# First attention of a two-layer cross-attention kernel: context halves of chunk 1 later in unit 0, two norms ahead of exponentials, the first addition to X ahead of a low half

## The chip, the cores and the metric

The kernel runs on one core of a Trainium2 chip. The metric is the device time of one execution in microseconds (us), the median of several runs. TensorE multiplies, ScalarE and VectorE work on SBUF and PSUM, GpSimd on SBUF, SyncE issues the DMAs. In the rows of the profile they are PE (PEld: its weight loads), ACT, DVE, POOL and SP.

## The reference, cut to what matters

```python
x = x + xattn0(layernorm(x), ctx, mask)   # 32 q heads, 8 kv heads, d 128, rotary
x = x + ffn0(layernorm(x))                # 4-bit weights
x = x + xattn1(layernorm(x), ctx)         # q and k normalised
x = x + ffn1(layernorm(x))                # routed, 512 wide
# xattn0, per batch of 64 tokens:
#   q, k = rope(x @ wq), rope(ctx @ wk); v = ctx @ wv
#   out = softmax(q k^T / sqrt(128) + mask) v @ wo
```

There are 32 batches of 64 tokens, 2048 tokens of width 512. The change touches the first attention (L = 0) alone.

## The kernel before, in words

Precision is kept by splitting each operand of a matmul into a high f16 part and a low f16 part, what the high part leaves over. Each product is three matmuls (high x high, high x low, low x high), so an output tile of 128 x 512 with depth 512 takes 12 matmuls. ScalarE makes most high parts (a copy with a conversion), VectorE most low parts (a subtraction).

**Units.** The tokens are in four chunks c of 512 (eight batches each), the heads in eight groups g of four query heads and one key and value head. A unit u is a pair (g, c); attention 0 has 32 of them. `UNITS` gives the order: (0,0), (1,0), (0,1), (1,1), (0,2), (1,2), (0,3), (1,3), and from there group by group. So chunk 1 of the context is first used by the keys of unit 2, chunk 2 by unit 4, chunk 3 by unit 6. Chunk c's layer norm is first used by the queries of those units.

**The pipeline.** Everything is written out by hand for each engine, and each engine runs its list strictly in order; semaphores join them. In step u (`units`, one function of this name per engine) the engines do the scores and softmax of unit u, the projections of unit u + 1 (`front(L, u + 1, beside=u)`), the output projection of unit u - 1 and then the weighted values of unit u:

- TensorE (`units`, L1292; `front`, L1277): `scores(u)` L934; `keys(u+1)` L865, `values(u+1)` L877; for each head h of four `queries(u+1, h)` L909; `turn_p` L943 (only for units 0 and 31; other units turn the weights by DMA, from SyncE); for t of four `output(u-1, t)` L957; `weigh(u)` L999.
- ScalarE (`units`, L1901; `front`, L1859): `turned_k` L1517 (halves of the key exchanged for the rotation), `exponent` L1599, `values_0` L1524, `keys_0` L1531, then per head `turned_q` L1538, and with a lag of two heads the high part `queries_0` L1545; `halved_p` L1609 in the middle. `weighed` L1629 at the start of the next step.
- VectorE (`units`, L2713; `front`, L2681): `weighed` L2331, `soft_max_0` L2255 to L2273, `turned_k` L2170, `soft_sum` L2309, `values_0` L2175, `keys_0` L2187, then per head `turned_q` L2182 and, lagging, the low part `queries_0` L2191. After the heads comes, for t of four, `output(u-1, t)` L2346, which adds the output tile in PSUM to X; between these are the low parts of the last two heads.
- GpSimd (`front`, L3090): the rotation's product with the sine L2953 and sum L2958 per head, the normalisation of the softmax L2964, the low parts of the weights L2973.

**Slots.** Other work is laid beside this with `plan(L, u, slot, stage, ...)`. Every engine calls `side(L, u, slot)` at ten fixed places of a step (0 ahead of the heads, 1 to 4 behind head 0 to 3, 5 to 8 behind output tile 0 to 3, 9 at the end), and `side` runs those planned stages that the engine has a part in. A stage name stands for different functions on different engines:

- `scale` of a context chunk or weight: on ScalarE the four high parts (L1480 for contexts, L1505 for weights). `low`: on VectorE two of the four low parts (L2127), for one half. Both read a staging area that one load fills; the next load of that area waits for the last low part.
- `ln_stats`: VectorE's statistics (L2133, L2139) and GpSimd's power and product (L2937, L2939). `ln_norm`: ScalarE writes the normalised rows of two of a chunk's four tiles (L1640). `ln_turn`: TensorE transposes them (L1028) and ScalarE takes the high parts (L1652). `ln_low`: VectorE takes the low parts (L2149).
- `peak`: TensorE, then VectorE find a power of two to scale by.

**PSUM banks.** `bank(i, ...)` makes TensorE wait until the readers of bank i's last content are through. The output tiles t = 0..3 use banks 2, 3, 0, 2, so that tile 3 waits for the addition of tile 0. `weigh` uses banks 0 and 1 first, so that it waits for the addition of tile 2. `ln_turn` uses banks 2 and 3 for the first two tiles of a chunk and 1 and 6 for the others, but for chunk 1 of this attention banks 2 and 3 both times.

In units 2, 4 and 30 (`LN_BESIDE`) ScalarE does the side stages of slot 5 ahead of the high part of head 3.

Of the kernel before, what the change touches and what calls it, by code (L numbers as in the profile page):

```python
# [87 lines left out]
def build(nc, din, out):  # L88
    ctx = ExitStack()
    with ctx:  # L90
# [330 lines left out]
        def plan(L, u, slot, *stage):  # L421
            SIDE.setdefault((L, u, slot), []).append(stage)
# [8 lines left out]
        def plan_ln(L, u, i, c, early=True, last=6):  # L431

            if early:
                plan(L, u - 1, 9, "ln_stats", i, c)
            for half, (norm, turn, low) in enumerate(((0, 2, 2), (3, 5, last))):
                plan(L, u, norm, "ln_norm", i, c, half)
                plan(L, u, turn, "ln_turn", i, c, half)
                plan(L, u, low, "ln_low", i, c, half)
# [6 lines left out]
                                                        ("low", key, 1))):  # L445
                plan(L, u, slot, *stage, *bank)

        for slot, *stage in ((1, "peak", ("c", 1), 2), (2, "scale", ("c", 1)), (2, "low", ("c", 1), 0), (9, "low", ("c", 1), 1)):
            plan(0, 0, slot, *stage)
        for slot, *stage in ((4, "ln_turn", 0), (4, "ln_norm", 1), (5, "ln_low", 0), (9, "ln_turn", 1), (9, "ln_low", 1)):  # L450
            plan(0, 0, slot, stage[0], 0, 1, *stage[1:])
        for u, slot, *stage in ((0, 1, "peak", w(0, 0, 2), 3), (0, 9, "scale", w(0, 0, 2)), (1, 0, "low", w(0, 0, 2), 0),
                                (1, 1, "low", w(0, 0, 2), 1)):
            plan(0, u, slot, *stage)
# [10 lines left out]
        for u in range(8, NU):  # L465
            g, c = UNITS[0][u]
# [6 lines left out]
        for u, slot, name, *a in ((26, 9, "gi", 1, 0), (27, 1, "gi", 1, 1), (27, 3, "gi", 1, 2), (27, 7, "zp", 1, 0), (27, 8, "zp", 1, 1),  # L473
                                  (27, 9, "zp", 1, 2), (28, 1, "zp", 0, 0), (28, 2, "zp", 0, 1), (28, 3, "zp", 0, 2),
                                  (28, 3, "gi", 0, 0), (28, 9, "gi", 0, 1), (29, 0, "gi", 0, 2)):
            plan(0, u, slot, name, *a)
        plan_ln(0, 30, 1, 0, last=7)
        for k, u, slot, hi in ((0, 29, 2, 3), (1, 29, 7, 5), (2, 30, 1, 7), (3, 30, 4, 0)):
            plan(0, u, slot, "unpack", 0, k)
            if hi:  # L480
# [11 lines left out]
        for u in range(8, NU):  # L492
            g, c = UNITS[1][u]
# [962 lines left out]
        def scalar(act):  # L1456
# [402 lines left out]
            def front(L, u, beside):  # L1859

                if L == 0:
                    if u > 1:
                        turned_k(u)
                    exponent(0, beside)
                    if u > 1:
                        values_0(u)
# [198 lines left out]
        def vector(dve):  # L2065
# [615 lines left out]
            def front(L, u, beside):  # L2681
                if (L, u) != (1, 1):
                    unit_scale(L, u)
                if L == 0:
                    if u > 1:
                        turned_k(u)
                    soft_sum(0, beside)
                    if u > 1:
                        values_0(u)
                    keys_0(u)  # L2690
                    side(0, beside, 0)
                    for h in range(4):
                        turned_q(u, h)
                        if (beside, h) == (0, 3):
                            turned_p(0, 0)
                        if h == 2:
                            halved_p(0, beside, 1)
                        if h in (2, 3):
                            queries_0(u, h - 2)
                        side(0, beside, 1 + h)  # L2700
                else:
                    if beside > 0:
                        values_1(u, 0)
                        soft_sum(1, beside)
                        values_1(u, 1)
                    else:
                        soft_sum(1, 0)
                    side(1, beside, 0)
                    for h in range(4):
                        queries_1(u, h)  # L2710
                        side(1, beside, 1 + h)

            def units(L):  # L2713
                for u in range(NU - 1):
# [13 lines left out]
                    for t in range(4):  # L2728
                        if u > 0:
                            output(L, u - 1, t)  # L2730
                        if L == 0 and t == 0:
                            queries_0(u + 1, 2)
                        if L and t == 1 and not k_by_dma(1, u + 1):
                            keys_1(u + 1)
# [529 lines left out]
```

## Time and profile before

| | us |
|---|---|
| median of 3 runs (2399.04 to 2400.89) | 2399.43 |
| the profiled execution | 2399.88 |
| its span, first to last instruction | 2398.1 |
| TensorE busy | 2349.9 |
| VectorE busy | 1740.3 |
| GpSimd busy | 1298.6 |
| ScalarE busy | 1290.0 |
| attention 0, until the last `weigh` of its steps | 0 to 965 |

The mean granted TensorE clock is 0.995 of 2.4 GHz. A row of the timeline has start (us from the span's start), duration of the merged group, engine, line, operation, what it writes and reads, count, and in brackets the idle time of the engine ahead of it with what released it. L numbers are those of the kernel before.

### The profile page before, as it was taken

How to read it: one execution, taken by the hardware profiler on the slowest of the kernel's cores; microseconds unless marked ns; L12 is line 12 of the kernel's file. 1: busy time of each engine (PE TensorE's matmuls, PEld its weight loads, DVE VectorE, ACT ScalarE, POOL GpSimd, SP SyncE). 2: the span in 40 equal slices, each digit the busy share in tenths (PEclk: the TensorE clock that was granted, in tenths of full speed). 3: DMA queues.
4: the chain of work that ended last, by engine and by line, in shares of the span. 5: the costliest groups of instructions: out<-in, count | busy, mean ns of one | idle time of the engine just before them, and what ended most of it. 6: DMA issues, size and time to landing. Idle time of an engine off the chain costs nothing.

```text
span 2398.1 us, 46211 instructions
## 1 busy us (share of the span) xinstructions
PE 2349.9 (98%) x18020; PEld 1329.5 (55%) x18028; DVE 1740.3 (73%) x3256; ACT 1290.0 (54%) x2511; POOL 1298.6 (54%) x1042
## 2 busy tenths in 40 slices
PE   8899999999999999999989999999999999999998
PEld 4555555555555555444666555555555555555554
DVE  8887887878787898756777576667666666766666
ACT  7666665656555555424444564555555555554453
POOL 4656566666666566237853354445555555445541
PEclk9999999999999999999999999999999999999999
DMA  6111121312121111011102111122121212221101
GB/s 213 45 45 36 45 54 27 124 27 54 32 56 29 43 40 29 27 44 36 35 21 69 58 32 28 45 54 63 36 63 36 63 36 62 54 43 27 27 14 71
DMA packets 217913, 116.60 MB, mean 49 GB/s; under 512 B 169409, under 2 KB 192609, under 8 KB 216673
## 3 DMA queue, kind: packets, MB, share of 16 engines
q1 hardware_dynamic: 217696, 113.64, 18.7%
q8 instruction: 145, 2.38, 0.4%
q14 instruction: 72, 0.58, 0.1%
HBM read 65.81 MB, written 8.39 MB: 31 GB/s over the span
## 4 chain that ended last, share of the span: by engine, by line
PE 55%; DVE 5%; ACT 2%; issue 1%; POOL 1%; DMA 0%; DVEq 0%; SPq 0%; ACTq 0%; POOLq 0%
PE PB L957 16%; PE PB L909 14%; PE PB L893 6%; PE PB L1069 4%; PE PB L1126 4%; PE PB L1080 3%; PE PB L934 2%; PE PB L999 2%; PE PB L978 1%; PE PB L1028 1%; DVE SML L2133 0%; PE PB L1223 0%; PE PB L1179 0%; DVE X L2489 0%; DVE X L2346 0%
## 5 line engine op out<-in xcount | busy, mean ns | idle before, releaser
L957 PE MATMUL PB<-WB,AR 128*128 128x512 f16 x3072 | 682.7, 379 | 2.5 <-DVE X L2346 2.3
L909 PE MATMUL PB<-XTB,WB 128*128 128x512 f16 x3072 | 678.9, 379 | 2.6 <-DVE WB L2127 1.5
L957 PEld LDWEIGHTS PB<-WB,AR 128*128 128x128 f16 x3072 | 296.7, 98 | 356.9 <-DVE X L2346 6.6
L909 PEld LDWEIGHTS PB<-XTB,WB 128*128 128x128 f16 x3072 | 297.5, 98 | 346.6 <-issue 6.2
L2964 POOL TENSOR_TENSOR AR<-AR,SML 128x512 f32<-128x512 f32 x128 | 144.7, 1152 | 314.4 <-DVE SML L2316 314.4
L2346 DVE SCALAR_TENSOR_TENSOR X<-PB,SML,X 128x512 f32<-128x512 f32 x256 | 188.9, 747 | 165.0 <-PE PB L957 159.0
L1629 ACT ACTIVATE AR<-PB 128x512 f16<-128x512 f32 x256 | 131.5, 598 | 231.7 <-PE PB L999 231.6
L2953 POOL TENSOR_TENSOR AR<-AR,CST 128x512 f32<-128x512 f32 x128 | 191.0, 1492 | 31.6 <-ACT AR L1539 31.6
L2220 DVE TENSOR_TENSOR AR<-PB,AR 128x512 f16<-128x512 f32 x128 | 88.2, 690 | 164.4 <-ACT AR L1592 164.4
L2958 POOL TENSOR_TENSOR AR<-AR 128x512 f32<-128x512 f32 x128 | 177.1, 1384 | 11.7 <-DVE AR L2182 1.9
L2944 POOL TENSOR_TENSOR AR<-AR,CST 128x512 f32<-128x512 f32 x32 | 46.7, 1460 | 237.3 <-ACT AR L1518 237.3
L1545 ACT ACTIVATE AR<-AR 128x512 f16<-128x512 f32 x128 | 80.7, 631 | 175.1 <-POOL AR L2958 173.6
L893 PE MATMUL PB<-WB,CTB 128*128 128x256 f16 x1536 | 173.1, 273 | 0.1
L2331 DVE TENSOR_TENSOR AR<-PB,AR 128x512 f16<-128x512 f32 x256 | 158.7, 683 | 13.3 <-ACT AR L1629 13.2
L2182 DVE TENSOR_TENSOR AR<-PB,CST 128x512 f32<-128x512 f32 x128 | 88.2, 689 | 107.6 <-ACT AR L1539 107.5
L3002 POOL TENSOR_TENSOR SML<-SML 128x16 f32<-128x16 f32 (+1 forms) x33 | 98.2, 2976 | 120.7 <-DVE SML L2228 120.7
L2191 DVE TENSOR_TENSOR AR<-AR 128x512 f16<-128x512 f32 x128 | 144.3, 1128 | 23.9 <-ACT AR L1545 23.9
L893 PEld LDWEIGHTS PB<-WB,CTB 128*128 128x128 f16 x1536 | 148.2, 98 | 17.4 <-DVE X L2346 0.4
L2994 POOL TENSOR_TENSOR AR<-AR 128x512 bf16<-128x512 f32 x128 | 146.9, 1157 | 16.1 <-ACT AR L1592 16.0
L2973 POOL TENSOR_TENSOR PSP<-AR,PSP 128x512 f16<-128x512 f32 x93 | 118.8, 1290 | 0.0
L934 PE MATMUL PB<-AR 128*128 128x64 f16 x3072 | 102.9, 194 | 3.2 <-DVE AR L2191 2.0
L934 PEld LDWEIGHTS PB<-AR 128*128 128x128 f16 x3072 | 95.7, 98 | 15.9 <-issue 14.3
(313 smaller groups left out, 4120.6 us busy)
## 6 DMA issues: line engine op xcount, KB each, us to landing
STG<-in_wo SPq DMA_DIRECT2D x14, 1024.0 KB
STG<-in_wq SPq DMA_DIRECT2D x13, 1024.0 KB
STG<-in_qw_gu SPq DMA_DIRECT2D x40, 128.0 KB
STG<-in_ctxT SPq DMA_DIRECT2D x4, 1024.0 KB
X<-in_x SPq DMA_DIRECT2D x4, 1024.0 KB, 10.4
kept<-CTB SPq DMA_DIRECT2D x4, 1024.0 KB, 7.3
CTB<-kept SPq DMA_DIRECT2D x4, 1024.0 KB, 6.4
out_x<-X SPq DMA_DIRECT2D x16, 256.0 KB, 2.4
```

The costliest lines, as they stand in the source:

```text
L893: m = pe.do.matmul(b[:, t2 * 256:(t2 + 1) * 256], CT[x][c][:, k, tok], wkv[y][:, k, :], start=n == 0, stop=n == 11)
L909: m = pe.do.matmul(b[:, :], wq[x][:, k, h * 128:(h + 1) * 128], XT[y][c][:, k, :], start=n == 0, stop=n == 11)
L934: m = pe.do.matmul(bk[:, b * SQ:(b + 1) * SQ], rows_of(QT[x], pair, b), KTT[y][:, b * SQ:(b + 1) * SQ], start=n == 0 and not by_pe, stop=n ...
L957: m = pe.do.matmul(b[:, :], AT[x][:, h, t * 128:(t + 1) * 128], wo[y][:, h, :], start=n == 0, stop=n == 11)
L1629: act.do.activation(hi, b[:, :].rearrange("p (b h q) -> p b h q", b=2, h=4), copy).then_inc(at_hi.of((L, u, j, odd)), 1)
L2191: dve.do.tensor_tensor(head_of(QT[1], h), by_batch(M1[h]), head_of(QT[0], h), ALU.subtract).then_inc(q_lo.of((0, u, h)), 1)
L2331: dve.do.tensor_tensor(lo, b[:, :].rearrange("p (b h q) -> p b h q", b=2, h=4), hi, ALU.subtract).then_inc(at_lo.of((L, u, j, odd)), 1)
L2346: dve.do.scalar_tensor_tensor(xs, PB[WB_OUT[t]][:, :], co(L, u, 0), xs, ALU.mult, ALU.add).then_inc(x_add.of((L, u, t)), 1)
L2953: pool.do.tensor_tensor(rt, rt, SINT.unsqueeze(1).to_broadcast([128, BC, SQ]), ALU.mult).then_inc(q_sin.of((u, h)), 1)
L2958: pool.do.tensor_tensor(M1[h], M1[h], RT[h], ALU.add).then_inc(q_add.of((u, h)), 1)
L2964: pool.do.tensor_tensor(v, v, RCT[:, cols].unsqueeze(2).to_broadcast([128, BC, SQ]), ALU.mult).then_inc(p_n.of((L, u, pair)), 1)
L2994: pool.do.tensor_tensor(head_of(SQL, h), by_batch(M1[h]), head_of(SQH, h), ALU.subtract).then_inc(sql.of((u, h)), 1)
```

## The change

Four edits, all in attention 0, none of which adds or removes an instruction:

1. In step 0 the high parts of context chunk 1 go from slot 2 to slot 4 (ScalarE; there behind `ln_turn` and `ln_norm`), and its first two low parts from slot 2 to slot 5 (VectorE; there behind `ln_low(0,1,0)`). The other two stay in slot 9.
2. The first `ln_norm` of chunks 2 and 3 (steps 2 and 4) goes from slot 0 to a new place "k" that only ScalarE has, ahead of `exponent`.
3. On VectorE, in steps 1 to 30, the low part of query head 1 goes from behind head 3 to behind `output(u-1, 0)`. In step 0, which has no output, it stays.
4. The second `ln_low` of the next norm (1, chunk 0) goes in step 30 from slot 7 to a new place "added" that only VectorE has, right behind `output(29, 0)`.

```diff
--- before.py
+++ after.py
@@ -432,7 +432,7 @@
 
             if early:
                 plan(L, u - 1, 9, "ln_stats", i, c)
-            for half, (norm, turn, low) in enumerate(((0, 2, 2), (3, 5, last))):
+            for half, (norm, turn, low) in enumerate((("k" if L == 0 and u < 5 else 0, 2, 2), (3, 5, last))):
                 plan(L, u, norm, "ln_norm", i, c, half)
                 plan(L, u, turn, "ln_turn", i, c, half)
                 plan(L, u, low, "ln_low", i, c, half)
@@ -445,10 +445,12 @@
                                                         ("low", key, 1))):
                 plan(L, u, slot, *stage, *bank)
 
-        for slot, *stage in ((1, "peak", ("c", 1), 2), (2, "scale", ("c", 1)), (2, "low", ("c", 1), 0), (9, "low", ("c", 1), 1)):
+        for slot, *stage in ((1, "peak", ("c", 1), 2), (9, "low", ("c", 1), 1)):
             plan(0, 0, slot, *stage)
         for slot, *stage in ((4, "ln_turn", 0), (4, "ln_norm", 1), (5, "ln_low", 0), (9, "ln_turn", 1), (9, "ln_low", 1)):
             plan(0, 0, slot, stage[0], 0, 1, *stage[1:])
+        plan(0, 0, 4, "scale", ("c", 1))
+        plan(0, 0, 5, "low", ("c", 1), 0)
         for u, slot, *stage in ((0, 1, "peak", w(0, 0, 2), 3), (0, 9, "scale", w(0, 0, 2)), (1, 0, "low", w(0, 0, 2), 0),
                                 (1, 1, "low", w(0, 0, 2), 1)):
             plan(0, u, slot, *stage)
@@ -474,7 +476,7 @@
                                   (27, 9, "zp", 1, 2), (28, 1, "zp", 0, 0), (28, 2, "zp", 0, 1), (28, 3, "zp", 0, 2),
                                   (28, 3, "gi", 0, 0), (28, 9, "gi", 0, 1), (29, 0, "gi", 0, 2)):
             plan(0, u, slot, name, *a)
-        plan_ln(0, 30, 1, 0, last=7)
+        plan_ln(0, 30, 1, 0, last="added")
         for k, u, slot, hi in ((0, 29, 2, 3), (1, 29, 7, 5), (2, 30, 1, 7), (3, 30, 4, 0)):
             plan(0, u, slot, "unpack", 0, k)
             if hi:
@@ -1861,6 +1863,7 @@
                 if L == 0:
                     if u > 1:
                         turned_k(u)
+                    side(0, beside, "k")
                     exponent(0, beside)
                     if u > 1:
                         values_0(u)
@@ -2695,8 +2698,9 @@
                             turned_p(0, 0)
                         if h == 2:
                             halved_p(0, beside, 1)
-                        if h in (2, 3):
-                            queries_0(u, h - 2)
+                            queries_0(u, 0)
+                        if h == 3 and beside == 0:
+                            queries_0(u, 1)
                         side(0, beside, 1 + h)
                 else:
                     if beside > 0:
@@ -2729,6 +2733,9 @@
                         if u > 0:
                             output(L, u - 1, t)
                         if L == 0 and t == 0:
+                            side(0, u, "added")
+                            if u > 0:
+                                queries_0(u + 1, 1)
                             queries_0(u + 1, 2)
                         if L and t == 1 and not k_by_dma(1, u + 1):
                             keys_1(u + 1)
```

## Rows read from the trace of the kernel before

**Rows 1.** The page: TensorE's busy time, and the costliest group of matmuls.

```profile
PE 2349.9 (98%) x18020; PEld 1329.5 (55%) x18028; DVE 1740.3 (73%) x3256; ACT 1290.0 (54%) x2511; POOL 1298.6 (54%) x1042
...
L957 PE MATMUL PB<-WB,AR 128*128 128x512 f16 x3072 | 682.7, 379 | 2.5 <-DVE X L2346 2.3
```

**Rows 2.** Timeline of TensorE, step 0 (columns as told above).

```profile
66.78 2.74 PE L999 MATMUL PB<-AR 64*128 64x256 f16 x24 [4.37 <-DVE AR L2321]
70.19 1.97 PE L1028 MATMUL PB<-CST,LNB 128*128 128x128 f32 x8 [0.67 <-DVE XTB L2149]
...
75.15 2.75 PE L865 MATMUL PB<-CTB,WB 128*128 128x512 f16 x12
```

**Rows 3.** Windows: length; busy us (x) of PE, PEld, DVE, ACT, POOL; granted clock; DMA.

```profile
65.30:75.50 10.20, 7.83 (x83) 6.44 (x85) 7.88 (x12) 7.84 (x14) 5.21 (x4) 0.53 0.08 15
119.90:123.30 3.40, 3.40 (x13) 1.59 (x12) 1.38 (x2) 3.31 (x7) 2.64 (x3) 0.59 0.00 0
```

**Rows 4.** Timeline of TensorE, steps 1 to 3.

```profile
101.94 1.49 PE L999 MATMUL PB<-AR 64*128 64x256 f16 x24 [0.53 <-DMA AR<-PSP]
...
118.71 1.79 PE L1028 MATMUL PB<-CST,LNB 128*128 128x128 f32 x8 [2.34 <-ACT LNB L1640]
...
141.29 2.75 PE L865 MATMUL PB<-CTB,WB 128*128 128x512 f16 x12
```

**Rows 5.** Timeline of TensorE, step 4.

```profile
181.60 1.33 PE L1028 MATMUL PB<-CST,LNB 128*128 128x128 f32 x8 [0.30 <-ACT LNB L1640]
```

**Rows 6.** Waits of TensorE in attention 0 (total, times, longest); step 8, TensorE and VectorE.

```profile
PE PB L957 <- DVE X L2346: 2.3, 5, 1.0
...
317.09 1.48 PE L999 MATMUL PB<-AR 64*128 64x256 f16 x24
...
311.77 1.54 DVE L2191 TENSOR_TENSOR AR<-AR 128x512 f16<-128x512 f32 x1
...
314.91 1.40 DVE L2346 SCALAR_TENSOR_TENSOR X<-PB,SML,X 128x512 f32<-128x512 f32 x2
```

**Rows 7.** Timeline of TensorE, step 30.

```profile
963.61 1.49 PE L999 MATMUL PB<-AR 64*128 64x256 f16 x24 [2.22 <-issue]
```

**Rows 8.** Timeline of ScalarE, step 0.

```profile
58.40 2.56 ACT L1480 ACTIVATE CTB<-STG,SML 128x512 f16<-128x512 f32 x4 [0.48 <-DVE SML L2095]
...
64.11 1.09 ACT L1616 ACTIVATE AR<-PB 128x512 f16<-128x512 f32 x2
...
66.56 1.53 ACT L1640 ACTIVATE LNB<-X,SML 128x512 f32<-128x512 f32 x2
...
72.69 2.55 ACT L1505 ACTIVATE WB<-XTB,SML 128x512 f16<-128x512 f32 x4
```

**Rows 9.** Timeline of VectorE, step 0.

```profile
59.84 3.32 DVE L2127 SCALAR_TENSOR_TENSOR CTB<-STG,SML,CTB 128x512 f16<-128x512 f32 x2
...
65.36 1.27 DVE L2321 TENSOR_TENSOR AR<-PB,AR 128x512 f16<-128x512 f32 x2
...
69.46 1.27 DVE L2149 TENSOR_TENSOR XTB<-PB,XTB 128x512 f16<-128x512 f32 x2
...
71.97 1.41 DVE L2127 SCALAR_TENSOR_TENSOR CTB<-STG,SML,CTB 128x512 f16<-128x512 f32 x2
...
75.75 2.48 DVE L2331 TENSOR_TENSOR AR<-PB,AR 128x512 f16<-128x512 f32 x4 [1.18 <-ACT AR L1629]
```

**Rows 10.** Timeline of GpSimd, steps 0 and 2.

```profile
59.66 1.28 POOL L2958 TENSOR_TENSOR AR<-AR 128x512 f32<-128x512 f32 x1
...
110.57 0.20 POOL L2939 TENSOR_TENSOR SML<-SML 128x4 f32<-128x4 f32 x1
```

**Rows 11.** Timeline of ScalarE, step 2.

```profile
114.50 1.34 ACT L1599 ACTIVATE AR<-AR,SML 128x512 f32<-128x512 f32 x2 [4.68 <-DVE AR L2273]
```

**Rows 12.** Timeline of VectorE, steps 2 and 30.

```profile
138.85 1.40 DVE L2127 SCALAR_TENSOR_TENSOR CTB<-STG,SML,CTB 128x512 f16<-128x512 f32 x2
...
960.15 1.40 DVE L2346 SCALAR_TENSOR_TENSOR X<-PB,SML,X 128x512 f32<-128x512 f32 x2
```

## The prediction

> **What bounds the kernel now.** I read the page's busy shares first: TensorE is busy for 98% of the span [rows 1]. So an edit can only bring what TensorE waits for, and what runs at a low clock. Then TensorE's waits by unit. Attention 0 is a chain of units; in a steady one TensorE waits for nothing, so VectorE, ScalarE and GpSimd count only where TensorE stands behind them. In reach of the change that is in five places. Unit 0: `weigh(0,0)` waits 4.37 us for VectorE's low half of the turned weights, and until the keys of chunk 1 the clock is low [rows 2, 3]. Unit 1: 0.53 us for the transposes, which end that unit's chain of softmax and GpSimd [rows 4]. Unit 2: 2.34 us for the norm of chunk 2, with a low clock behind it [rows 3, 4]. Unit 4: 0.30 us for the norm of chunk 3 [rows 5]. Five later units: 2.3 us together where the fourth output tile waits for the first addition to X, whose bank it takes [rows 6]. Unit 30 has 2.22 us at `weigh` [rows 7].
>
> **1. Context halves of chunk 1, unit 0.** ScalarE's four high parts (2.56 us) [rows 8] leave slot 2 for slot 4, two of VectorE's low parts (3.32 us) [rows 9] for slot 5. No instruction is added. What follows in ScalarE's queue then moves up, but only to where GpSimd's sum of head 0 ends, 60.94 [rows 10]; rotation 3 goes 61.6 to 62.8 and the turned weights start at 62.85 instead of 64.11 [rows 8]. VectorE no longer carries 3.32 us of halves, takes its two subtractions (1.27) [rows 9] behind the first copy, and ends them at 64.75 instead of 66.63: `weigh(0,0)` starts 1.9 us earlier.
>
> That is not where unit 0 ends. ScalarE's high parts now stand between `ln_norm(0,1,1)`, which ended at 68.09 [rows 8] and now ends near 66.9, and the high part of query head 2. They run to 69.4, that head's high part is ready near 70.05 instead of 68.6, and VectorE, idle since about 65.3, makes its low part to 70.7. Behind it in the queue stands `ln_low(0,1,0)`, which before began at 69.46 [rows 9]: now 70.7. TensorE's second turn of the norm (70.19 before) [rows 2] waits for the bank that the first tile frees: 71.5. From there to `keys(2)` were 4.96 us [rows 2]; with the wait for the second bank a little less: 76.2 instead of 75.15, **+1.05**. VectorE meanwhile: halves 0 (1.41, the row of the same two instructions with GpSimd idle) [rows 9], head 3, halves 1, `ln_low`, done by 76.4. ScalarE turns the norm once TensorE has (73.5), to 74.2, then writes `wo`'s high parts (2.55, at 72.69 before) [rows 8] from 74.1, so `weighed` starts near 76.6 and VectorE's four subtractions at 77.1 instead of 75.75 [rows 9]: **+1.4**. They are followed without a gap by the softmax of unit 1, GpSimd's normalisation and the transposes for which `weigh(0,1)` already waited 0.53. TensorE, 1.05 late, has no slack of 1.4: unit 1 ends **1.4 us later**. Bounds: 0, if TensorE's turn runs at full clock and the wait at GpSimd's sum closes; +3.3, if the moved halves still take 3.32. SyncE's next load of that staging area (chunk 2) leaves some 2 us later, ahead of unit 1's transposes; its first reader is ScalarE's square in slot 9 of unit 1, so this costs nothing.
>
> Two instructions of low parts took 3.32 us beside GpSimd and 1.41 us with GpSimd idle [rows 9, 10], and this is why I take 1.41 behind 71.9, where GpSimd has nothing. The Trainium skill (SBUF — State Buffer, "Who interferes with whom") says that a VectorE instruction with two inputs in SBUF and a GpSimd instruction that reads SBUF exclude each other. By that rule the moved halves are free of it (+1.4); without it they would stay at 3.32 and the unit at +3.3.
>
> **2. Norms ahead of exponentials, units 2 and 4.** Two activations (1.53 us) [rows 8] go ahead of exponentials for which ScalarE stood idle 4.68 us in unit 2 [rows 11]; GpSimd has the statistics ready by 110.8 [rows 10], so the norm ends at 112.3, before 114.50, and costs nothing. TensorE's turn is at hand at 116.4 and no longer waits 2.34; without that stall the stretch of 3.40 us at a mean clock of 0.59 (levels 1.2 and 2.4 GHz) [rows 3] should go: 3.40 x 0.41 = 1.4. On TensorE 3.7 us. Next late is VectorE: its queue starts 1.4 us earlier (ScalarE has 1.5 less ahead of the rotations). Walking its queue in the order of the code, with the durations that it had, I get the low parts of chunk 2 done at 138.6, where they ended at 140.25 [rows 12]. `keys(4)` needs them and began at 141.29 [rows 4]; TensorE would be there at 137.6. So **-2.7**, between -1.7 (if VectorE gives 0.65 of its 1.65) and -3.7. Unit 4: the wait of 0.30 and the gap between its two tiles (the turn took 1.33 there [rows 5]): **-0.7**, -0.3 to -0.9; ScalarE is idle ahead of those exponentials too.
>
> **3. First addition ahead of a low half, 30 units; unit 30.** VectorE makes the addition before the low half of head 1 (1.54) [rows 6], so the bank is free 1.5 us earlier. All five waits, 2.3 us [rows 6], go, and each gives back an overlap of 379 - 222 = 157 ns (682.7 us over 3072) [rows 1]: at most 3.1. But `weigh` needs the third addition, which does not move: in the unit with the longest wait (1.0) it ended at 316.31, and `weigh` came at 317.09 [rows 6], so that only 0.7 of 1.2 comes back. The short ones bring 1.8, less 0.6 in units where the third addition is by then just in time: **-1.9**, -0.9 to -3.1. VectorE would stall only where it reached the addition before TensorE ended the first output tile. In that unit three tiles of 12 matmuls, 8.0 us, and the wait lie between that and 317.09: it ended near 308.0, and VectorE comes to the addition at 311.8 [rows 6], 3.8 us after. In unit 30 the profile names no releaser; by the code `weigh` waits there for the bank that the second `ln_low` empties. That comes 4 us earlier now, but pushes back the third addition, for whose bank `weigh` waits too: it ended at 961.55 [rows 12], and with two `ln_low` (1.27) and one low half ahead and head 3 behind it comes near 963.3, against `weigh` at 963.61 [rows 7]: **-0.1**, +0.5 to -0.8.
>
> Sum: 1.4 - 2.7 - 0.7 - 1.9 - 0.1 = **-4.0 us**. The profiled execution took 2399.88 (span 2398.1); the median of the three runs shown is 0.45 lower, 2399.43. So 2395.4. A measurement of this kernel can tell about 0.2%, 4.8 us, from no change: the line lies at 2394.6, close by.
>
> **Rivals.** (a) *VectorE closes up*: chunk 2's low parts are ready when TensorE comes, and all five waits go. For it: the same pair of VectorE instructions takes 1.41 or 3.32 us [rows 9], by what GpSimd does, so its queue may shorten by more than I give it. Against: GpSimd's own queue moves along with it. 1.4 - 3.7 - 0.9 - 3.1 - 0.5 = -6.8: **2392.6**. (b) *Unit 0 costs more*: halves still stretched, or the low clock lasts into the keys, +3.3: sum -2.1, **2397.3**. For it: between TensorE's last transpose near 62.4 and 71.5 there is only one `weigh`. (c) *The gain moves to the third addition*: nothing from part 3: -2.1, **2397.3**. (d) *The other side: slower.* The place is VectorE's wait for TensorE's first output tile, in each of 29 units, with the low halves of heads 1 and 2 queued behind it and the next scores behind those. If it stalls 0.3 us per unit beyond what VectorE's gaps take, that is 8.7, and -4.0 + 1.9 + 8.7 = +6.6: **2406.0**. It decides from a stall of some 0.24 us per unit. Against: the 3.8 us above. (e) *It doesn't do what it says*: the norm of unit 2 doesn't run before the exponentials, because its statistics (VectorE, then GpSimd) are late; they had 3.7 us to spare [rows 10, 11]. Without part 2's gain in unit 2: -1.3, **2398.1**.
>
> **How the numbers follow.** Forecast 0.52, within 1.5 us of it; (a) 0.18, (b) 0.12, (c) 0.09, (d) 0.05, (e) 0.04. The forecast is its likeliest case's: 2395.4. The range reaches to (a) with its bounds below and to (b) and (c) above, leaves out (d), and takes in the spread of the runs shown: 2392.4 to 2398.6. Faster by over 0.2% is (a) and a third of the forecast's own spread: 0.36; within it 0.59; slower 0.05.
>
> **What would show it.** In unit 0 `weigh` starts near 64.9, TensorE then stands about 4 us ahead of the second turn, `weigh(0,1)` near 103.3. In unit 2 the wait for the norm is gone, the clock stays full, and a new wait of about 1 us ahead of `keys(4)` names VectorE's context halves. No wait of an output tile for an addition is left in attention 0, and `weigh` in the unit of 317 waits for one instead. I'm wrong if unit 1 ends earlier than before, if `keys(4)` doesn't wait, or if the gain shrinks steadily from unit 5 to unit 30.

## The result, and the profile after

The changed kernel takes 2407.55 us (2406.46 to 2408.6, 6 runs) against 2399.61 (2398.88 to 2400.89, 6 runs) for the one before on the same chip: ratio 1.0029, 95% interval 1.0019 to 1.0039. That is 8 us slower, where I forecast 4.0 us faster. The profiled execution took 2408.49 with a span of 2406.7, against 2399.88 and 2398.1.

The page's busy times of the kernel after:

```profile
PE 2352.1 (98%) x18028; PEld 1330.1 (55%) x18028; DVE 1759.1 (73%) x3256; ACT 1289.9 (54%) x2511; POOL 1284.5 (53%) x1042
```

VectorE is the row to look at against [rows 1]: the same 3256 instructions are busy for 1759.1 us instead of 1740.3. Instructions that were only moved have become longer. What TensorE waits for up to 975 us (total, times, longest):

```profile
PE PB L1001 <- DVE X L2349: 12.2, 16, 1.6
PE PB L1030 <- DVE XTB L2152: 4.8, 1, 4.8
...
PE PB L1001 <- DVE AR L2324: 1.6, 1, 1.6
...
PE PB L867 <- DVE CTB L2130: 0.6, 1, 0.6
```

(In the kernel after, `weigh` is L1001, `output` L959 and VectorE's addition L2349, its low half L2194, `queries` L911, `keys` L867, `ln_turn` L1030.) The wait of [rows 6], an output tile for the first addition, is gone, as meant. In its place `weigh` waits in 16 units for an addition, 12.2 us together. The groups of instructions say which of VectorE's have grown (busy us, mean ns of one). The query heads' low halves of the kernel before:

```profile
L2191 DVE TENSOR_TENSOR AR<-AR 128x512 f16<-128x512 f32 x128 | 144.3, 1128 | 23.9 <-ACT AR L1545 23.9
```

and of the kernel after:

```profile
L2194 DVE TENSOR_TENSOR AR<-AR 128x512 f16<-128x512 f32 x128 | 168.6, 1332 | 17.8 <-ACT AR L1547 17.6
```

They alone are 24.3 us more. GpSimd is busy for 14.1 us less than before (1284.5 against 1298.6 [rows 1]): part of the time for which one engine held up the other has moved from GpSimd's instructions into VectorE's. Unit 18, a steady one, shows how. VectorE and GpSimd of the kernel before:

```profile
601.59 1.53 DVE L2191 TENSOR_TENSOR AR<-AR 128x512 f16<-128x512 f32 x1
...
603.40 0.75 DVE L2346 SCALAR_TENSOR_TENSOR X<-PB,SML,X 128x512 f32<-128x512 f32 x1
604.07 0.74 DVE L2191 TENSOR_TENSOR AR<-AR 128x512 f16<-128x512 f32 x1
604.73 1.40 DVE L2346 SCALAR_TENSOR_TENSOR X<-PB,SML,X 128x512 f32<-128x512 f32 x2
...
602.54 1.72 POOL L2953 TENSOR_TENSOR AR<-AR,CST 128x512 f32<-128x512 f32 x1
604.34 1.61 POOL L2958 TENSOR_TENSOR AR<-AR 128x512 f32<-128x512 f32 x1
...
607.17 1.05 PE L999 MATMUL PB<-AR 64*128 64x256 f16 x16
```

and of the kernel after:

```profile
606.10 0.75 DVE L2349 SCALAR_TENSOR_TENSOR X<-PB,SML,X 128x512 f32<-128x512 f32 x1
606.77 3.40 DVE L2194 TENSOR_TENSOR AR<-AR 128x512 f16<-128x512 f32 x2
610.09 1.40 DVE L2349 SCALAR_TENSOR_TENSOR X<-PB,SML,X 128x512 f32<-128x512 f32 x2
...
606.69 1.27 POOL L2960 TENSOR_TENSOR AR<-AR,CST 128x512 f32<-128x512 f32 x1
608.03 1.59 POOL L2965 TENSOR_TENSOR AR<-AR 128x512 f32<-128x512 f32 x1
...
611.55 0.72 PE L1001 MATMUL PB<-AR 64*128 64x256 f16 x10 [0.89 <-DVE X L2349]
```

Before, the low half of head 1 runs beside GpSimd (1.53), then the addition stands in between, and the low half of head 2 starts at 604.07, just before GpSimd changes from one instruction to the next (its product ends at 604.26, its sum starts at 604.34). It takes 0.74, and GpSimd's sum behind it 1.61. After, the two follow each other from 606.77, while GpSimd is busy from 606.69 to 609.62 without a gap, and take 3.40 together instead of 2.27. Twenty of the 30 units have such a pair of 3.4 us. From the end of the last rotation product the third addition ends 5.75 us later (605.74 to 611.49) instead of 4.54 (601.59 to 606.13), though the same instructions stand between them. That is 1.21 us, and the third addition had been only 1.04 early (606.13 against 607.17).

How long such a subtraction takes can be told from where it starts. I take the low halves that start more than 0.15 us before the end of a GpSimd instruction: in 92 of 93 cases in the kernel before, and in 89 of 90 in the kernel after, the low half lasts what that instruction still had to run, plus 0.54 to 0.56 us. The two of unit 18 above started with some 1.2 us of a GpSimd instruction to run, and took 1.73 and 1.75.

The 1.21 against 1.04 us would leave a wait of 0.17, and `weigh` waits 0.89. The other 0.7 come from unit 17, whose third addition was late too. VectorE starts the softmax work of unit 18 about 0.5 us later behind `weigh` of unit 17 than before, and a pair of subtractions in it, which are not low halves, meets GpSimd in another way. Before and after:

```profile
585.16 1.29 DVE L2273 TENSOR_TENSOR AR<-AR,SML 128x512 f32<-128x512 f32 x2
...
589.10 1.84 DVE L2276 TENSOR_TENSOR AR<-AR,SML 128x512 f32<-128x512 f32 x2
```

Before, the pair starts 0.06 us after a GpSimd instruction, and that one is held up (2.48 us). After, it starts 0.58 us behind it, GpSimd takes 1.27, and the pair is stretched. Counted from `weigh` of unit 17 (578.20 before, 581.62 after) the pair ends 1.07 us later than before, ScalarE's exponentials start 1.07 later, and the last rotation product ends 0.73 later.

Time from `weigh` to `weigh`, from the timelines, against what I forecast:

| | before | after | difference | forecast |
|---|---|---|---|---|
| start of `weigh` of unit 1 | 101.94 | 104.59 | +2.65 | +1.4 |
| unit 2 | 36.09 | 33.41 | -2.68 | -2.7 |
| unit 3 | 29.40 | 30.13 | +0.73 | 0 |
| unit 4 | 31.85 | 31.09 | -0.76 | -0.7 |
| unit 5 | 28.97 | 28.97 | 0 | 0 |
| units 6 to 29 | 700.88 | 708.29 | +7.41 | -1.9 |
| unit 30 | 34.48 | 33.59 | -0.89 | -0.1 |
| rest of the span | 1434.5 | 1436.6 | +2.1 | 0 |

(The row of a unit is the time from the `weigh` before to its own.) Unit 4 came as forecast. Unit 2 came to the forecast figure, but not in the forecast way: see edit 2 alone, below. TensorE of the kernel after, step 0 and step 2:

```profile
66.44 1.49 PE L1001 MATMUL PB<-AR 64*128 64x256 f16 x24 [1.59 <-DVE AR L2324]
72.69 1.97 PE L1030 MATMUL PB<-CST,LNB 128*128 128x128 f32 x8 [4.76 <-DVE XTB L2152]
...
118.88 0.60 PE L1030 MATMUL PB<-CST,LNB 128*128 128x128 f32 x4
120.54 0.63 PE L1030 MATMUL PB<-CST,LNB 128*128 128x128 f32 x4 [1.06 <-issue]
...
138.00 1.48 PE L1001 MATMUL PB<-AR 64*128 64x256 f16 x24 [0.36 <-DVE X L2349]
...
141.99 1.24 PE L867 MATMUL PB<-CTB,WB 128*128 128x512 f16 x5 [0.57 <-DVE CTB L2130]
```

In step 2 the turn no longer waits 2.34 for ScalarE [rows 4], but its second tile comes 1.06 behind the first, for which the profile names no releaser, and `keys(4)` waits 0.57 for the context halves. This `keys(4)` stands behind `weigh` of unit 2, so its delay is in the row of unit 3: from 138.00 to 141.99 are 3.99 us, from 138.03 to 141.29 before 3.26. In step 0 the wait ahead of `weigh` fell from 4.37 to 1.59, and 4.76 appeared at the second turn. Unit 1 needs care: `turn_p` of unit 0, ahead of all that was moved, stands at 62.94 instead of 60.50, so that execution is 2.4 us late before the change can act. How much of this reaches `weigh` of unit 1, whose wait at the `weigh` before takes up part of it, is worked out below. TensorE was at its low clock at another moment in that execution (from 58 to 68 us at a mean of 1.00 of 2.4 GHz, where the one before had 0.83).

### The profile page after: what moved, and what is told of

The parts are those of the page before. It is cut to its first block, busy times and chain, and to the rows that moved or that the text cites. A ratio compares the mean times of both kernels' runs of the same rounds, so it can differ in the third digit from the quotient of the medians.

```text
span 2406.7 us, 46219 instructions
## 1 busy us (share of the span) xinstructions
PE 2352.1 (98%) x18028; PEld 1330.1 (55%) x18028; DVE 1759.1 (73%) x3256; ACT 1289.9 (54%) x2511; POOL 1284.5 (53%) x1042
## 4 chain that ended last, share of the span: by engine, by line
PE 53%; DVE 5%; ACT 2%; POOL 1%; issue 1%; DMA 0%; DVEq 0%; SPq 0%; ACTq 0%; POOLq 0%
PE PB L959 15%; PE PB L911 13%; PE PB L895 6%; PE PB L1071 4%; PE PB L1128 4%; PE PB L1082 3%; PE PB L936 2%; PE PB L1001 2%; PE PB L980 1%; PE PB L1030 1%; DVE SML L2136 0%; PE PB L1225 0%; PE PB L1181 0%; DVE X L2349 0%; DVE X L2492 0%
## 5 line engine op out<-in xcount | busy, mean ns | idle before, releaser
L911 PE MATMUL PB<-XTB,WB 128*128 128x512 f16 x3072 | 680.2, 380 | 2.3 <-DVE WB L2130 1.2
L959 PE MATMUL PB<-WB,AR 128*128 128x512 f16 x3072 | 681.5, 379 | 0.2
L959 PEld LDWEIGHTS PB<-WB,AR 128*128 128x128 f16 x3072 | 297.5, 98 | 352.6 <-issue 2.6
L911 PEld LDWEIGHTS PB<-XTB,WB 128*128 128x128 f16 x3072 | 297.7, 98 | 347.0 <-issue 7.4
L2349 DVE SCALAR_TENSOR_TENSOR X<-PB,SML,X 128x512 f32<-128x512 f32 x256 | 188.4, 745 | 162.0 <-PE PB L959 156.0
L2960 POOL TENSOR_TENSOR AR<-AR,CST 128x512 f32<-128x512 f32 x128 | 179.2, 1400 | 29.7 <-ACT AR L1541 29.7
L2194 DVE TENSOR_TENSOR AR<-AR 128x512 f16<-128x512 f32 x128 | 168.6, 1332 | 17.8 <-ACT AR L1547 17.6
L2951 POOL TENSOR_TENSOR AR<-AR,CST 128x512 f32<-128x512 f32 x32 | 44.3, 1384 | 252.5 <-ACT AR L1520 252.5
L1001 PE MATMUL PB<-AR 64*128 64x256 f16 x1536 | 95.1, 270 | 14.7 <-DVE X L2349 12.2
```

What stands on the lines that cost most here:

```text
L911: m = pe.do.matmul(b[:, :], wq[x][:, k, h * 128:(h + 1) * 128], XT[y][c][:, k, :], start=n == 0, stop=n == 11)
L959: m = pe.do.matmul(b[:, :], AT[x][:, h, t * 128:(t + 1) * 128], wo[y][:, h, :], start=n == 0, stop=n == 11)
L1001: m = pe.do.matmul(bk[odd][:, jj * 256:(jj + 1) * 256], vd[x][rows, b2, :], PT[y][rows, :, b2, :], start=n == 0, stop=n == 2)
L2194: dve.do.tensor_tensor(head_of(QT[1], h), by_batch(M1[h]), head_of(QT[0], h), ALU.subtract).then_inc(q_lo.of((0, u, h)), 1)
L2349: dve.do.scalar_tensor_tensor(xs, PB[WB_OUT[t]][:, :], co(L, u, 0), xs, ALU.mult, ALU.add).then_inc(x_add.of((L, u, t)), 1)
L2960: pool.do.tensor_tensor(rt, rt, SINT.unsqueeze(1).to_broadcast([128, BC, SQ]), ALU.mult).then_inc(q_sin.of((u, h)), 1)
```

## Experiments

**Which edit costs it.** Theory A: VectorE and GpSimd exclude each other, and edit 3 lets one more low half meet GpSimd. The first four kernels are parts of the change; the kernel before took 2400.4 us beside them.

Edit 3 alone:

```diff
-                        if h in (2, 3):
-                            queries_0(u, h - 2)
+                        if h == 2:
+                            queries_0(u, 0)
+                        if h == 3 and beside == 0:
+                            queries_0(u, 1)
...
                         if L == 0 and t == 0:
+                            if u > 0:
+                                queries_0(u + 1, 1)
                             queries_0(u + 1, 2)
```

> Edit 3 alone: the first addition to X ahead of the low half of head 1, everything else as before. Theory A (VectorE takes the low halves of heads 1 and 2 back to back while GpSimd works, both are stretched, and the third addition, for whose bank weigh waits, comes about 1 us later): +7 us against before (+5.5 to +9), with some 15 waits of weigh for an addition, 11 to 13 us in total, and VectorE's low halves of query heads at a mean of 1.33 us instead of 1.13. Rival B (the loss is made in steps 0 to 2 and by the clock at both ends, and edit 3 only shows it): within 2 us of before. Rival C (VectorE stalls for the first output tile): slower too, but with idle time of VectorE ahead of the first addition in most steps, and no longer low halves.

Measured: 2409.64 us (2408.57 to 2410.38, 5 runs), ratio 1.0035 (1.0022 to 1.0049). Its group of low halves:

```profile
L2191 DVE TENSOR_TENSOR AR<-AR 128x512 f16<-128x512 f32 x128 | 169.6, 1340 | 15.3 <-ACT AR L1545 15.3
```

and, of TensorE's waits, that of `weigh` for an addition:

```profile
PE PB L999 <- DVE X L2346: 10.1, 14, 1.4
```

Units 6 to 29 take 708.14 together. The loss is 9.2 us, a little more than the 5.5 to 9 expected, with a little less of the waits (10.1 us where I expected 11 to 13). This edit holds the whole loss. It does not yet say by what mechanism.

Edits 1, 2 and 4, without edit 3 (against the changed kernel):

```diff
-                            queries_0(u, 0)
-                        if h == 3 and beside == 0:
-                            queries_0(u, 1)
+                        if h in (2, 3):
+                            queries_0(u, h - 2)
...
-                            if u > 0:
-                                queries_0(u + 1, 1)
                             queries_0(u + 1, 2)
```

> The change without edit 3: context halves, norms, and the norm's second low half in step 30. Theory A: what the changed kernel gained in steps 2, 4 and 30 (2.7 + 0.8 + 0.9) stays and steps 5 to 29 cost nothing, against some 1.4 to 2.6 lost in steps 0 and 1: -2 us against before (-4 to 0), and the five waits of an output tile for an addition are back. Rival B: +1 to +3, because the loss is in these edits.

Measured: 2398.67 us (11 runs: ten from 2396.43 to 2400.03, and one of 7362.43), ratio 0.9989 (0.998 to 0.9998). Low halves 142.7 us (mean 1116 ns), units 6 to 29 700.85: as before the change. Step 2 takes 32.98 here, step 3 29.40.

Edit 1 alone:

```diff
-        for slot, *stage in ((1, "peak", ("c", 1), 2), (2, "scale", ("c", 1)), (2, "low", ("c", 1), 0), (9, "low", ("c", 1), 1)):
+        for slot, *stage in ((1, "peak", ("c", 1), 2), (9, "low", ("c", 1), 1)):
...
+        plan(0, 0, 4, "scale", ("c", 1))
+        plan(0, 0, 5, "low", ("c", 1), 0)
```

> Edit 1 alone: the context halves of chunk 1 later in step 0. Forecast's own term: +1.4 us (0 to +3.3), weigh of step 0 up to 1.9 us earlier, the second turn of the norm 1.3 later with a wait of 4 to 5 us ahead of it, weigh of step 1 later by 1.4. Rival: the whole 2.65 us by which weigh of step 1 was late in the changed kernel is edit 1's: +2.65. A second rival: most of it was where the low clock fell, ahead of the moved work: +0.5 or less.

Measured: 2402.58 us (2401.82 to 2405.98, 11 runs), ratio 1.0012 (1.0003 to 1.002). That is 2.2 us slower, with `weigh` of unit 1 at 103.48, 1.5 later than before.

Edit 2 alone:

```diff
-            for half, (norm, turn, low) in enumerate(((0, 2, 2), (3, 5, last))):
+            for half, (norm, turn, low) in enumerate((("k" if L == 0 and u < 5 else 0, 2, 2), (3, 5, last))):
...
+                    side(0, beside, "k")
                     exponent(0, beside)
```

> Edit 2 alone: the norms of chunks 2 and 3 ahead of the exponentials of steps 2 and 4. Theory: step 2 shorter by 2.7 us (36.09 to about 33.4) with a wait of 0.5 to 1 us for the context halves ahead of the keys of unit 4, step 4 by 0.7; -3.4 us against before (-2.4 to -4.6). Rival: VectorE's queue gives the time back in step 3: -1.5 or less.

Measured: 2397.46 us (2395.36 to 2399.45, 11 runs), ratio 0.9987 (0.9978 to 0.9996). Step 2 takes 32.98, step 4 31.09: -3.1 and -0.8. The wait of 0.5 to 1 us ahead of the keys of unit 4 that I expected did not come, neither here nor in the kernel without edit 3. TensorE in step 2 and at `keys(4)`, with edit 2 alone:

```profile
117.69 0.60 PE L1028 MATMUL PB<-CST,LNB 128*128 128x128 f32 x4
119.35 0.63 PE L1028 MATMUL PB<-CST,LNB 128*128 128x128 f32 x4 [1.06 <-issue]
...
139.64 2.75 PE L865 MATMUL PB<-CTB,WB 128*128 128x512 f16 x12
```

So edit 2 alone brings 3.1 us, and TensorE does not wait for VectorE's context halves, which end at 139.41. The wait of 0.57 at `keys(4)` and that of 0.36 at `weigh` of unit 2 are there only with edit 3 beside it, whose low halves of heads 1 and 2 together take 3.05 us in that unit.

**By what mechanism.** The next kernels take an instruction away from GpSimd, or change only VectorE's order; the kernel before took 2400.6 us beside them. In the first two GpSimd's product of head 3 with the sine is left out in units 2 to 31 (they leave this term of the rotation out):

```diff
+                if h == 3 and u > 1:
+                    return
                 pool.do.tensor_tensor(rt, rt, SINT.unsqueeze(1).to_broadcast([128, BC, SQ]), ALU.mult).then_inc(q_sin.of((u, h)), 1)
...
-                pool.wait_ge(q_sin, (u, h))
+                if h < 3 or u < 2:
+                    pool.wait_ge(q_sin, (u, h))
```

With edit 3:

> Edit 3, and GpSimd's product with the sine of head 3 is left out in the units 2 to 31 of the first attention (that head's queries are rotated wrongly). Theory A: only one of the two low halves behind the first addition still starts while GpSimd works, the third addition comes about 1 us earlier than with edit 3 alone, and the waits of weigh for an addition fall from 10 to 12 us to under 2. Against the kernel before +0 us (-3 to +2). Rival C (the order of the additions against TensorE's tiles sets it, not GpSimd): the waits stay at 8 us or more.

Measured: 2396.12 us (2393.65 to 2399.45, 11 runs), ratio 0.9984 (0.9975 to 0.9992). This is 4.5 us faster, more than the 3 at most that I expected; one wait of `weigh` for an addition is left in units 2 to 30, of 0.56.

Without edit 3:

> The kernel before with the same product of GpSimd left out (that head's queries are rotated wrongly), to compare the run above with. Theory A: -1 to -4 us against before; edit 3 on top of it costs at most 2 us where it cost 8.4 on the whole kernel. Rival C: edit 3 costs some 8 us on top of it all the same.

Measured: 2398.73 us (2397.07 to 2400.3, 11 runs), ratio 0.9992 (0.9983 to 1.0001). With one GpSimd instruction fewer, edit 3 brings 2.6 us where it cost 9.2 with that instruction (2409.64 against 2400.4). The intervals of the two ratios overlap, so that the gain is not sure, but a loss of 9 is excluded. In the profiles units 6 to 29 take 697.99 against 699.21 here, and 708.14 against 700.88 with the instruction. Unit 18 of the kernel with edit 3 and less GpSimd:

```profile
600.43 0.75 DVE L2346 SCALAR_TENSOR_TENSOR X<-PB,SML,X 128x512 f32<-128x512 f32 x1
601.10 2.34 DVE L2191 TENSOR_TENSOR AR<-AR 128x512 f16<-128x512 f32 x2
603.36 1.40 DVE L2346 SCALAR_TENSOR_TENSOR X<-PB,SML,X 128x512 f32<-128x512 f32 x2
...
599.79 2.50 POOL L2965 TENSOR_TENSOR AR<-AR 128x512 f32<-128x512 f32 x2
...
605.98 1.27 PE L999 MATMUL PB<-AR 64*128 64x256 f16 x20
```

The same two low halves in the same order take 2.34 us instead of 3.40, because GpSimd is done at 602.29. So it is GpSimd that stretches them, not their order or ScalarE: the first starts with 1.19 us of a GpSimd instruction to run and takes 1.74, the second takes 0.68.

Now the order alone, with all of GpSimd's work: VectorE adds the first tile, makes the low half of head 1, adds the second and third tile, and makes the low halves of heads 2 and 3 last. In step 0, which has no output tiles, this order also puts `ln_low(0,1,0)` and whatever else is in slot 5 ahead of the low half of head 2. The expectation of the kernel with all four edits, below, says "in units 1 to 30" and passes over this. Against edit 3 alone:

```diff
                                 queries_0(u + 1, 1)
-                            queries_0(u + 1, 2)
...
                         if L == 0 and t == 2:
+                            queries_0(u + 1, 2)
                             queries_0(u + 1, 3)
```

> Edit 3 with the low half of head 2 also moved, behind the third addition (VectorE: first addition, low half 1, second and third addition, low halves 2 and 3). Theory A: the third addition is ready some 1.7 us earlier than with edit 3 and no longer late; the low half of head 2 then runs when GpSimd is through, 0.68 us instead of 1.7. Neither weigh nor an output tile waits for an addition: -3 us against before (-4 to 0). Rival: VectorE now stands at the third addition until TensorE's tile is there, ends the step later, and the wait goes to the scores or to the next step's queries: +1 or more.

Measured: 2398.77 us (2396.24 to 2400.94, 11 runs), ratio 0.9993 (0.9984 to 1.0001). Its unit 18:

```profile
600.20 0.75 DVE L2346 SCALAR_TENSOR_TENSOR X<-PB,SML,X 128x512 f32<-128x512 f32 x1
600.86 1.75 DVE L2191 TENSOR_TENSOR AR<-AR 128x512 f16<-128x512 f32 x1
602.53 1.47 DVE L2346 SCALAR_TENSOR_TENSOR X<-PB,SML,X 128x512 f32<-128x512 f32 x2
603.92 1.28 DVE L2191 TENSOR_TENSOR AR<-AR 128x512 f16<-128x512 f32 x2
...
602.14 1.60 POOL L2962 TENSOR_TENSOR AR<-AR 128x512 f32<-128x512 f32 x1
```

and its group of low halves:

```profile
L2191 DVE TENSOR_TENSOR AR<-AR 128x512 f16<-128x512 f32 x128 | 143.4, 1139 | 3.6 <-ACT AR L1545 3.6
```

The low half of head 1 is still stretched (1.75). The additions, which read one operand from PSUM, stand beside GpSimd and take 1.47 for two; the low halves come when GpSimd is done and take 1.28 for two. No wait of TensorE's for an addition is left in units 5 to 29, at an output tile or at `weigh` (one of 0.2 us is left, at a `keys`), and units 6 to 29 take 697.76 together, 3.12 less than before: the upper end that I had given part 3. The whole kernel's median shows 1.8 of the 3 that were expected, and the interval does not exclude none. In the profiled execution unit 30 took 0.5 longer (34.96) and the rest of the span 2.1 (1436.6). That rest lies anywhere between 1434.5 and 1437.7 us in the thirteen profiled executions. TensorE's program is the same in all of them there. Some of the spread can be read right at its start: from `weigh` of unit 30 to the next output tile TensorE takes 3.04 us in most, 4.4 in three that run partly at the low clock there (this one, edit 3 alone, edit 2 alone: 0.88 over the 14 us behind that `weigh`), and 4.02 in the three executions further below that have this order and edit 4 together, where that tile waits 1.03 for VectorE. What sets the remainder stays open.

That order with edits 2 and 4 beside it, without edit 1 (against the kernel above):

```diff
-            for half, (norm, turn, low) in enumerate(((0, 2, 2), (3, 5, last))):
+            for half, (norm, turn, low) in enumerate((("k" if L == 0 and u < 5 else 0, 2, 2), (3, 5, last))):
...
-        plan_ln(0, 30, 1, 0, last=7)
+        plan_ln(0, 30, 1, 0, last="added")
...
+                    side(0, beside, "k")
...
+                            side(0, u, "added")
```

> The order of VectorE above with edits 2 and 4 of the change and without edit 1 (context halves as before). If the parts add up: -3 from the norms, -1 from step 30, -3 from the additions: -7 us against before (-4 to -9), faster than both kernels. Rival (they share one slack): no better than the norms alone, -3.

Measured: 2392.85 us (2390.93 to 2395.03, 6 runs), ratio 0.9965 (0.9953 to 0.9977). This beats both kernels. Unit 30 takes 32.63, 1.85 less than before, and `weigh` waits for nothing there; 1.0 of that is lost again to the wait of 1.03 behind it. The same kernel was measured a second time, beside the two that follow, where the kernel before took 2401.0 us.

> The kernel with edits 2 and 4 and the order addition 0, low half 1, additions 1 and 2, low halves 2 and 3, once more with more runs: its first measurement was 2392.85, ratio 0.9965 (0.9953 to 0.9977), from 6 runs. If that holds, 2391.5 to 2394; if it was a lucky draw, 2395 or above, since the terms give 2400 - 2.7 - 0.7 - 3.1 - 0.9 = 2392.6.

Measured: 2394.3 us (2392.53 to 2395.07, 8 runs), ratio 0.9973 (0.9963 to 0.9983). The gain is there a second time, 6.7 us after 7.7; the median lies between my two cases, just above the first.

All four edits with that order (against the kernel above):

```diff
-        for slot, *stage in ((1, "peak", ("c", 1), 2), (2, "scale", ("c", 1)), (2, "low", ("c", 1), 0), (9, "low", ("c", 1), 1)):
+        for slot, *stage in ((1, "peak", ("c", 1), 2), (9, "low", ("c", 1), 1)):
...
+        plan(0, 0, 4, "scale", ("c", 1))
+        plan(0, 0, 5, "low", ("c", 1), 0)
```

> All four edits of the change, but in units 1 to 30 VectorE's order is addition 0, low half of head 1, additions 1 and 2, low halves of heads 2 and 3, so that the low halves no longer meet more of GpSimd's instructions than before and the third addition is not held up. Theory A (the loss sits in the order of VectorE alone, and the other edits keep what they brought): the kernel with edits 2 and 4 and this order took 2392.85, and edit 1 cost +1.0 to +1.2 where it could be read: 2394, between 2392 and 2396; no wait of weigh for an addition in units 5 to 29, steps 6 to 29 at 697.8 together. Rival B (edit 1 pays once VectorE's queue is no longer the late one): 2392 or below, unit 1 ending no later than 102.2. Rival C (part of the loss comes with edit 1 through VectorE's queue): 2398 or above.

Measured: 2393.44 us (2391.95 to 2394.62, 8 runs), ratio 0.9971 (0.996 to 0.9981), units 6 to 29 at 697.77. Against the changed kernel it differs only by where VectorE's low half of head 2 stands, and the loss of 8 us is a gain of 7.6. The profiled executions are 14.8 us apart: 10.5 of it is in units 6 to 29, and 3.0 ahead of `weigh` of unit 1. For the latter the order in step 0 counts. VectorE and TensorE there:

```profile
66.48 1.27 DVE L2152 TENSOR_TENSOR XTB<-PB,XTB 128x512 f16<-128x512 f32 x2
68.46 2.69 DVE L2130 SCALAR_TENSOR_TENSOR CTB<-STG,SML,CTB 128x512 f16<-128x512 f32 x2 [0.71 <-ACT CTB L1482]
...
68.54 1.27 PE L1030 MATMUL PB<-CST,LNB 128*128 128x128 f32 x8
```

`ln_low(0,1,0)` no longer stands behind the low half of head 2, and the second turn follows `weigh` without the 4.76. The moved context halves meet GpSimd and take 2.69 instead of 1.40. Rival C falls. Of rival B the sign in unit 1 came (101.57, not later than 102.2) with the order in step 0, and the time did not (2392 or below). With edit 1 this order takes 0.9 us less than without it (2394.3), which these runs don't tell apart.

Edit 4 alone:

```diff
-        plan_ln(0, 30, 1, 0, last=7)
+        plan_ln(0, 30, 1, 0, last="added")
...
+                            side(0, u, "added")
```

> Edit 4 alone: the second ln_low of chunk 0 for attention 1 is made behind the first addition of unit 30 in place of slot 7. Forecast of the prediction -0.1 (+0.5 to -0.8); with edits 1 and 2 beside it, step 30 took 33.57 against 34.48. Theory A: step 30 takes 33.6 here too, and the kernel 0.9 less than the one before, which the runs can't tell from none. Rival: step 30 stays at 34.5, and the 0.9 came with the others' later position of the low clock.

Measured: 2399.37 us (2398.17 to 2402.8, 11 runs), ratio 0.9994 (0.9986 to 1.0003). Unit 30 takes 33.60: 0.9 less than before, as theory A had it.

## Why the prediction was wrong

**The step that failed** is in part 3: "`weigh` needs the third addition, which does not move". It moves. The unit that I took this from, with `weigh` at 317.09, shows it after the change:

```profile
312.97 3.42 DVE L2194 TENSOR_TENSOR AR<-AR 128x512 f16<-128x512 f32 x2
316.31 1.40 DVE L2349 SCALAR_TENSOR_TENSOR X<-PB,SML,X 128x512 f32<-128x512 f32 x2
...
317.76 1.48 PE L1001 MATMUL PB<-AR 64*128 64x256 f16 x24 [1.41 <-DVE X L2349]
```

The third addition ends at 317.71 where I had it at 316.31; only 0.18 of this is there ahead of the additions, at VectorE's last rotation product. I had assumed that instructions which change places within a queue leave the sum of their durations alone. Here one of the two low halves was short (0.73) only because the addition between them carried it to the end of a GpSimd instruction. In units 6 to 29 the term was -1.9, with bounds of -0.9 to -3.1; it measured +7.4. The bounds held no loss at all, though this was the same pair of rows, 3.32 against 1.41 for two such instructions [rows 9, 10], from which I had argued in part 1. I priced the exclusion where the context halves were moved and not where the low half was moved, 30 times over. A small slip beside it: the four short waits and their overlaps come to 1.9, not 1.8, which would make the term -2.0.

The Trainium skill (SBUF — State Buffer, "Who interferes with whom") says that a VectorE instruction with two inputs in SBUF contends with a GpSimd instruction that reads SBUF. The pairs of 3.40 and 2.34 us agree with it.

**The rivals.** Slower by 6.6 was (d), at 0.05. The side and the size were near, the mechanism was not: VectorE does not stall for the first output tile (it starts the addition at 606.10 directly behind its own work). What `weigh` waits for was named in (c), which let it swallow a gain and not make a loss. Of (a), that the halves of chunk 2 are ready when TensorE comes is what edit 2 alone shows; in the changed kernel edit 3 undoes it.

**Part 2** was right in what it takes away, the wait of 2.34 and the low clock behind it, and in unit 4 (-0.76 against -0.7). That unit 2 shows -2.68 where I had -2.7 is luck. I had 3.7 on TensorE, less 1.0 because VectorE's context halves would be late at `keys(4)`. Counted from `weigh` of unit 1, I had the halves ready after 36.7 us and TensorE there after 35.7. With edit 2 alone the halves are ready after 36.0 and TensorE starts `keys(4)` after 36.2. The walk through VectorE's queue took the durations that it had, and the low half of head 2 takes 0.74 there where it had 1.34, so the same assumption failed here in the other direction; and TensorE's 3.7 lacks the 1.06 between the turn's tiles. The term is -3.1. In the changed kernel edit 3 takes 0.4 of it at `weigh` of unit 2, and 0.7 more in unit 3: `keys(4)`, for which I had forecast -2.7, is early by 1.95 against `weigh` of unit 1.

**Part 1** was right in mechanism: `weigh` earlier, then 4.76 us at the second turn, the moved halves at 1.40 with GpSimd idle. Its size depends on when the low clock falls, so I compare kernels by where `turn_p` of unit 0 starts. At 62.9 to 63.9, `weigh` of unit 1 starts at 103.32 to 103.40 in three kernels without edit 1 and at 104.39 and 104.59 in two with it: +1.0 to +1.3. At 62.0 to 62.5 it is 101.93 to 102.01 in three without it and 103.48 with it alone: +1.5. The forecast was +1.4. In the order of VectorE that adds three tiles first, edit 1 costs nothing: `weigh` of unit 1 starts at 101.79 and 102.13 without it and at 101.57 with it. That is not the clock's doing but the order's, because the wait of 4.76 is not there. Of the changed kernel's +2.65 some 1.4 are there without edit 1 in the kernels that start alike, and so not the change's.

**Unit 30** measured -0.9 where I had -0.1, outside my bound of -0.8: `weigh` does wait there for the third addition, as I had it, 1.3 us with edit 4 alone and 1.59 in the changed kernel, but that is less than the 2.22 [rows 7] which it waited for the bank of `ln_low`. The mechanism held and the term was mis-sized. With the third addition ahead of the low half as well, unit 30 gave -1.85.

**What adds up.** 2.65 - 2.68 + 0.73 - 0.76 + 7.41 - 0.89 + 2.1 = 8.6 us between the two profiled executions, which differ by 8.61 (2408.49 - 2399.88); the medians differ by 7.94. Unit 3's +0.73 appears only where edits 2 and 3 stand together: the unit takes 29.40 us with edit 3 alone, with edit 2 alone, and with edits 1, 2 and 4. Of the 2.1 of the rest, 1.7 are in the last 20 us. TensorE in the tail of the kernel after:

```profile
2389.28 1.71 PE L1225 MATMUL PB<-STG,XTB 128*128 128x512 f32 x2 [1.25 <-DVE X L2644]
2390.79 1.91 PE L1232 MATMUL PB<-X,CST 128*128 128x512 f32 x2
...
2393.65 2.74 PE L1225 MATMUL PB<-STG,XTB 128*128 128x512 f32 x6
```

and of the kernel before:

```profile
2382.39 1.13 PE L1223 MATMUL PB<-STG,XTB 128*128 128x512 f32 x2 [1.25 <-DVE X L2641]
2383.35 1.02 PE L1230 MATMUL PB<-X,CST 128*128 128x512 f32 x2
...
2385.07 2.74 PE L1223 MATMUL PB<-STG,XTB 128*128 128x512 f32 x6
```

The same matmuls take 4.37 us from the first row to the last of these, and 2.68 before. The granted clock is 0.66 from 2389 to 2394 us, and 1.00 from 2382 to 2386 before.

## What to carry to other kernels

The duration of an instruction in the trace belongs to its place: before moving one, look at what GpSimd is doing at the new place, and price its neighbours' durations there too, not only its own. For the low halves here the price could be read off the timeline: what is left of GpSimd's instruction when VectorE's starts, plus 0.55 us. Where the two hold each other up, put VectorE's instructions with one input in PSUM beside GpSimd's and the ones with two inputs in SBUF into its gaps. And when a wait for one instruction is shortened by moving it ahead, check how much slack the next one in that queue has: here 1.04 us, and the stretch was 1.21. A late end is carried into the next unit, where it can meet GpSimd again. And a term that comes out at its forecast size in the whole is not confirmed until its edit has run alone: unit 2's did so by errors that cancelled.

## What the runs showed of the hardware

In unit 18 a subtraction with both inputs in SBUF took 0.67 to 0.74 us where GpSimd was idle or about to end an instruction, and 1.53 to 1.75 where it started inside one, while an addition with one input in PSUM took 0.73 to 0.75 in either place. Over the kernel there are values between, by how much of GpSimd's instruction was left. In the same kernels GpSimd's sum mostly takes 1.27 or 1.60, its product 1.27 or 1.72. What I had not expected is how much a step can lose by it: with 1.1 us more on VectorE, busy 73% of the time, a unit of 28.97 us became 29.93.

The moment at which TensorE's low clock falls in the first 130 us is not the same from one kernel to the next, even where they agree up to there: `turn_p` of unit 0 started anywhere from 60.50 to 63.87 us, and in the six kernels that keep the order of step 0 and lack edit 1, `weigh` of unit 1 anywhere from 101.93 to 103.40. A difference of one us at the first units is not an effect until kernels with the same start are compared.
